# Transposing an fp32 state in one pass and splitting it out of PSUM, in place of transposing its two fp16 halves

## The reference

```python
state = x
for _ in range(5):
    s_in = state @ in_W.T + in_b
    s_out = state @ out_W.T + out_b
    a = concatenate([adj @ s_in, adj.T @ s_out, state])
    r = sigmoid(a @ r_W.T + r_b)
    z = sigmoid(a @ z_W.T + z_b)
    joined = concatenate([adj @ s_in, adj.T @ s_out, r * state])
    h_hat = tanh(joined @ h_W.T + h_b)
    state = (1 - z) * state + z * h_hat
out = tanh(state @ o1_W.T + o1_b) @ o2_W.T + o2_b
return layernorm(x + out)
```

## Time and profile before

| | us |
|---|---|
| median of 3 runs | 1097.2 (1095.56 to 1097.23) |
| profiled execution, first to last instruction (its span) | 1094.1 |
| median less span | 3.1 |
| TensorE busy | 1070.0 |
| VectorE busy | 582.4 |
| ScalarE busy | 249.8 |
| GpSimd busy | 22.4 |

### The profile page before, as it was taken

One profiled execution on the slowest core, in us unless ns is written; L12 is line 12 of the kernel. 1 busy time (PEld: TensorE's weight loads), 2 busy tenths in 40 slices (PEclk: granted clock), 3 DMA queues, 4 the chain that ended last, 5 costly groups with the idle time before them and its releaser, 6 DMA issues.

```text
span 1094.1 us, 12578 instructions
## 1 busy us (share of the span) xinstructions
PE 1070.0 (98%) x5160; PEld 497.1 (45%) x5160; DVE 582.4 (53%) x1024; ACT 249.8 (23%) x314; POOL 22.4 (2%) x27
## 2 busy tenths in 40 slices
PE   6999999999999999999999999999999999999994
PEld 3444444444444444444444444444444444444442
DVE  5944478854443536271726262635445363747466
ACT  3666322221211111121112112112121121111111
POOL 0300000020000000000000000000000000101000
PEclk9999999999999999999999999999999999999998
DMA  9989100010000000000000000000000000101000
GB/s 339 398 309 398 67 1 1 1 39 1 1 1 1 1 1 1 2 1 1 1 1 1 1 1 2 1 1 1 1 1 1 1 1 1 39 1 39 1 20 19
DMA packets 13638, 46.30 MB, mean 42 GB/s; under 512 B 1168, under 2 KB 7952, under 8 KB 9488
## 3 DMA queue, kind: packets, MB, share of 16 engines
q1 hardware_dynamic: 13584, 45.49, 10.9%
HBM read 43.39 MB, written 2.10 MB: 42 GB/s over the span
## 4 chain that ended last, share of the span: by engine, by line
PE 95%; DVE 2%; DMA 1%; SPq 1%; ACT 1%; issue 0%; DVEq 0%
PE bank L646 50%; PE bank L724 42%; PE bank L737 1%; DMA tmp<-in_adj 1%; PE bank L766 1%; PE bank L748 1%; SPq L196 0%; DVE deg_words L477 0%; ACT tmp L307 0%; DVE tmp L502 0%; ACT a L270 0%; DVE pq_words L418 0%; SPq L193 0%; SPq L192 0%; DVE pq_words L574 0%
## 5 line engine op out<-in xcount | busy, mean ns | idle before, releaser
L724 PE MATMUL bank<-pq_words,w 128*128 128x512 f16 x1440 | 327.6, 379 | 0.0
L646 PE MATMUL bank<-a,state_n 128*128 128x512 fp8e4 x1280 | 280.8, 379 | 3.3 <-ACT a L270 3.3
L646 PE MATMUL bank<-at_words,state_n 128*128 128x512 fp8e4 x1280 | 282.0, 379 | 0.2
L418 DVE SCALAR_TENSOR_TENSOR pq_words<-bank,pq_words 128x512 f16<-128x512 f32 x80 | 55.2, 691 | 350.2 <-ACT pq_words L297 328.1
L724 PEld LDWEIGHTS bank<-pq_words,w 128*128 128x128 f16 x1440 | 140.8, 98 | 168.3
L646 PEld LDWEIGHTS bank<-at_words,state_n 128*128 128x128 f16 x1280 | 124.6, 98 | 149.4 <-issue 1.1
L646 PEld LDWEIGHTS bank<-a,state_n 128*128 128x128 f16 x1280 | 124.3, 98 | 150.0 <-issue 3.9
L307 ACT ACTIVATE tmp<-tmp,bias_sb,scal 128x512 f32<-128x512 f32 x120 | 97.3, 813 | 394.4 <-DVE tmp L502 394.4
L724 PE MATMUL bank<-split_t,w 128*128 128x512 f16 x480 | 116.7, 379 | 0.6 <-DVE deg_words L477 0.6
L502 DVE TENSOR_TENSOR tmp<-bank,tmp 128x512 f32<-128x512 f32 x120 | 82.5, 689 | 57.4 <-PE bank L724 56.6
L297 ACT ACTIVATE pq_words<-bank 128x512 f16<-128x512 f32 x64 | 38.2, 597 | 315.0 <-PE bank L646 315.0
(11 more groups left out here) (90 smaller groups left out, 383.2 us busy)
## 6 DMA issues: line engine op xcount, KB each, us to landing
tmp<-in_adj SPq DMA_DIRECT2D x16, 1024.0 KB, 6.8
tmp<-in_adj_t SPq DMA_DIRECT2D x16, 1024.0 KB, 6.9
pq_words<-in_gate_w SPq DMA_DIRECT2D x6, 384.0 KB, 6.1
at_words<-in_x SPq DMA_DIRECT2D x4, 512.0 KB, 8.4
state_t<-in_x_t SPq DMA_DIRECT2D x4, 512.0 KB, 7.7
pq_words<-in_x SPq DMA_DIRECT2D x4, 512.0 KB, 4.2
out<-pq_words SPq DMA_DIRECT2D x8, 256.0 KB, 2.3
deg_words<-in_io_w SPq DMA_DIRECT2D x4, 128.0 KB, 4.0
```

The costliest lines, as they stand in the source:

```text
L418: return nc.vector.scalar_tensor_tensor(pq[:, c, q, 1, :], src[:, :], PSC, pq[:, c, q, 0, :], ALU.mult, ALU.subtract).then_inc(done, 1)
L646: return nc.tensor.matmul(dst[:, :], state_n[:, j, part, feat(f)], adj8[:, j, cols(c)], start=j == 0 and part == 0, stop=j == JT - 1 and p ...
L724: last = nc.tensor.matmul(dst[:, :], w16[:, k, wp, feat(gi)], rhs, start=i == 0 and (wp, xp) == PASSES[0], stop=i == KT - 1 and (wp, xp) = ...
```

## The change

Each group of 8 fp16 transposes becomes 4 fp32 transposes of `state_t` itself, with a new fp32 identity `ident32`, into the same bank, read as 128x512 in fp32 (`tr32`). ScalarE makes the hi half out of the bank, with the scale. A new VectorE instruction, `nat_lo`, makes the lo half out of the bank and the hi half, and counts the new semaphore `s_natl`. TensorE's waits move from `s_sl` to `s_new` and from `s_nat` to `s_natl`. On VectorE `nat_lo` stands: at the start of steps 1 to 4 (both feature tiles of chunk 3), behind `pq_lo` 0 and 1 of chunks 1 to 3 in steps 1 to 3, and in the first step's chunks 1 to 3 between `gate_pre` and `update` of gate tiles 4 and 5. GpSimd makes `ident32` with one copy.

```diff
+        ident32 = sb("ident32", [P, P], F32)
...
-        tr16 = tr_bank[:, :].bitcast(F16).rearrange("p (j s f) -> p j s f", j=JC, s=2)
+        tr32 = tr_bank[:, :].rearrange("p (j f) -> p j f", j=JC)
...
+            pool.wait_ge(s_const, 2)
+            nc.gpsimd.tensor_copy(ident32[:, :], ident[:, :]).then_inc(s_id32, 1)
...
             def nat_out(n, c, f, direct):
                 dst = state_n if direct or c == CH - 1 else next_n
                 act.wait_ge(s_tr, 2 * n + f + 1)
-                nc.scalar.copy(dst[:, c * JC:(c + 1) * JC, :, feat(f)], tr16).then_inc(s_nat, 1)
+                nc.scalar.activation(dst[:, c * JC:(c + 1) * JC, 0, feat(f)], tr32, ACT.Identity, scale=SIG) \
+                    .then_inc(s_nat, 1)
...
-            def gates(n, c):
+            def nat_lo(n, c, f, direct):
+                dst = state_n if direct or c == CH - 1 else next_n
+                rows = dst[:, c * JC:(c + 1) * JC, :, feat(f)]
+                dve.wait_ge(s_nat, 2 * n + f + 1)
+                nc.vector.scalar_tensor_tensor(rows[:, :, 1, :], tr32, SIG, rows[:, :, 0, :],
+                                               ALU.mult, ALU.subtract).then_inc(s_natl, 1)
+
+            def gates(n, c, between=False):
...
                 for f in range(FT):
                     gate_pre(n, 2 * FT + f)
+                    if between:
+                        nat_lo(n - 1, c - 1, f, True)
                     update(n, c, f)
...
-            def step(t, last):
+            def step(t, last, first_direct):
                 for c in range(CH):
                     n = CH * t + c
+                    if c == 0:
+                        nat_lo(n - 1, CH - 1, 0, first_direct)
+                        nat_lo(n - 1, CH - 1, 1, first_direct)
                     pq_lo(n, 0)
+                    if c > 0 and not last:
+                        nat_lo(n - 1, c - 1, 0, False)
...
                     pq_lo(n, 1)
+                    if c > 0 and not last:
+                        nat_lo(n - 1, c - 1, 1, False)
...
-                        dve.wait_ge(s_nat, 2 * n)
+                        dve.wait_ge(s_natl, 2 * n)
...
             for c in range(CH):
-                gates(c, c)
+                gates(c, c, between=c > 0)
...
             def transposes(n, c, f):
-                pe.wait_ge(s_sl, FT * n + f + 1)
+                pe.wait_ge(s_new, FT * n + f + 1)
                 if isinstance(n, int) and n == 0 and f == 0:
                     pe.wait_ge(s_deg, 2 * CH)
+                    pe.wait_ge(s_id32, 1)
                 else:
-                    pe.wait_ge(s_nat, 2 * n + f)
+                    pe.wait_ge(s_natl, 2 * n + f)
                 for j in range(JC):
-                    for part in range(2):
-                        last = nc.tensor.transpose(tr16[:, j, part, :],
-                                                   split_t[:, part, f, c * CW + j * P:c * CW + (j + 1) * P],
-                                                   ident[:, :])
+                    last = nc.tensor.transpose(tr32[:, j, :],
+                                               state_t[:, f, c * CW + j * P:c * CW + (j + 1) * P],
+                                               ident32[:, :])
                 last.then_inc(s_tr, 1)
...
                     if c == 0:
-                        pe.wait_ge(s_nat, 2 * n)
+                        pe.wait_ge(s_natl, 2 * n)
...
-            pe.wait_ge(s_nat, 2 * (CH - 1))
+            pe.wait_ge(s_natl, 2 * (CH - 1))
             start_step(CH - 1)
```

More of the change, by code:

```diff
@@ L137, in gnn_program @@
         s_cast = sem("s_cast")
-        s_const0, s_const = sem("s_const0"), sem("s_const")
+        s_const0, s_const, s_id32 = sem("s_const0"), sem("s_const"), sem("s_id32")
         s_mx, s_mall = sem("s_mx"), sem("s_mall")
@@ L155, in gnn_program @@
         s_sh, s_sl = sem("s_sh"), sem("s_sl")
-        s_tr, s_nat = sem("s_tr"), sem("s_nat")
+        s_tr, s_nat, s_natl = sem("s_tr"), sem("s_nat"), sem("s_natl")
         s_cur = sem("s_cur")
@@ L624, in _ @@
             for c in range(CH):
-                gates(c, c)
+                gates(c, c, between=c > 0)
             with dve.Fori(1, STEPS - 1) as t:
-                step(t, False)
-            step(STEPS - 1, True)
+                step(t, False, True)
+            step(STEPS - 1, True, True)
         @block.tensor
```

## The result

The changed kernel takes 1109.12 us (median of 4 runs, 1106.82 to 1110.06) against 1097.12 us: 1.011 times the kernel before, 95% interval 1.0095 to 1.0124. It is slower by 12.0 us. The forecast was 1104.5 us, 7.4 us slower: the direction and the range held, the size was 4.6 us short. The profiled execution has a span of 1106.7 us and took 1108.51, so 1.8 us lie around a span. The 3.1 us that the forecast put there for the kernel before also held 1.3 us by which its profiled execution was shorter than the median.

The account below looks back on a forecast made before the run. The prediction took TensorE to bound the kernel: 7.9 us of first-step waits plus 29 x (0.43 - 0.45) gave +7.3 us on a 1094.1 us span, 1101.4, and with 3.1 around it 1104.5 us; range 1097.5 to 1117.5.

Parts of the forecast that it names:

- The 3.1 us: Time around the profiled span: the median of the runs was put 3.1 us above the 1094.1 us span.
- TensorE as the bound: TensorE holds 95% of the chain; each nanosecond its transposes take or it waits there is a nanosecond of the kernel.
- Part 1: Transposes on TensorE: a group of 4 fp32 ones takes 0.43 us against 0.45 for 8 fp16; 29 groups count.
- transpose mode four times faster for fp32: Cited for the cheap-transpose rival: 54 ns per fp32 transpose, no more than an fp16 one; 1098.4 us, chance 0.18.
- Part 2: ScalarE and VectorE in steps 1 to 4: VectorE gets 22 us more work, none of it on the path.
- Part 3: First step's gates: TensorE waits for `nat_lo` four times, 2.56, 1.87, 1.87 and 1.64 us, 7.9 us in sum.
- Nor should the granted clock fall in a wait of 2.5 us: First step's waits: TensorE keeps the full 2.4 GHz clock, as 19 matmuls did after 3.30 us of idling.
- The forecast's own range of 1103 to 1106 us: Range around the main case of 1104.5 us, which was given chance 0.56.
- the stated range: 1097.5 to 1117.5 us, from just under the cheap-transpose case to the upper end of the dear-transpose case.

Follow-up runs that it names:

- e2_double: e1_early with each group of four fp32 transposes issued twice; 1110.31 us, 1.0117 times the kernel before.
- e3_fp16_wait: Kernel before, keeping fp16 transposes, with a VectorE copy of the lo half at each place of `nat_lo`, TensorE waiting for it; 1103.43 us, 1.0063 times the kernel before.
- e0_again: The changed kernel run again, unchanged, on a second chip; 1106.69 us, 1.0098 times the kernel before.
- e4_first_only: Changed kernel with only the first lo half of each of the first step's chunks made earlier; 1103.51 us, 1.0060 times the kernel before.
- e6_copy_only: Kernel before with only GpSimd's copy of the identity to fp32 added, which nothing reads; 1097.11 us, 1.0004 times the kernel before.
- e1_early: Changed kernel with the first step's lo halves made earlier on VectorE, second hi half earlier on ScalarE; 1099.72 us, 1.0035 times the kernel before.
- e8_early_again: e1_early run again, for a second profile and more timed runs; 1100.21 us, 1.0025 times the kernel before.

## Why the prediction was right in direction and short in size

- TensorE as the bound: right. From `start_step` to the last gate tile the time follows the transposes' price alone, -0.42 us measured, 26 x (0.435 - 0.45) = -0.39. One reading was loose: the last transposes of the earlier trace rows start at 869.5, 0.5 us behind the stretch of the earlier trace rows; nothing hangs on it.
- Part 1, the price of an fp32 group: right, 0.44 us for 0.43. Four transposes of a row take 0.60 us with a tail of 0.27, so one comes each 0.11 us, twice an fp16 one. The loads last 140 ns and don't set the pace: in e2_double 8 of them take 1.01 us, 0.12 from start to start, so that they overlap. By the Trainium skill, page "TensorE: Matmul & The Clock Gate", section "Weight-path perf modes — Fast Weight Load (FWL) and DoubleRow", fp32 gets no fast load. The 140 against 98 ns fit that, but the group was not bound by it. The Trainium skill, page "TensorE: Matmul & The Clock Gate", section "Terms", has transpose mode four times faster for fp32. Taken against two passes as L641's products are made in, the rows show half: 0.11 us, where two passes of 128 columns are 0.217 us, an estimate from L641's 256 columns.
- Part 2, no cost from the second step on: right. 270 to 881 us has 0.14 us of idle time.
- Part 3, the four waits: right in place, releaser and size, 2.60, 1.98, 1.99 and 1.67 us for 2.56, 1.87, 1.87 and 1.64. `nat_lo` took 0.75, not 0.69 us; `nat_out` took 0.68, within the 0.60 to 0.81.
- The step that failed: "Nor should the granted clock fall in a wait of 2.5 us". It was read from a single row in which the clock had held behind 3.30 us of idling. In the profile after it fell behind 2.45 us in the first step (1.7 us lost), behind 3.75 at the start (1.7 us) and behind 2.74 at the end, in e3_fp16_wait behind 2.11; in e0_again it held behind 2.46. The length of the idle time doesn't decide it: at the start it fell behind 2.08 us (e4_first_only) and held behind 3.49 (e6_copy_only). Whether it falls differs from run to run, and I had left the term out instead of bounding it. The forecast's own range of 1103 to 1106 us failed by it; the stated range held because it was made wide for the price of the transposes, which wasn't what was off.
- That term is also where the 12 us differ from 7.4: of the 5.3 us by which the span was over its forecast, 0.3 us are the waits' size, 0.2 the smaller saving on the groups, and 4.8 the three stretches at the lower clock, less the small shifts of start and end beside them. The runs bear out that it is a matter of what follows idle times, since holding TensorE busy at the ends took 2.5 to 3.6 us off e1_early. Why the changed kernel falls more often at the ends than the kernel before, with TensorE's order there the same, stays open. If the mean clocks of the timed runs mean what those of the profiles do, it is the end above all: all 7 runs of e8_early_again are at 0.993, but 50 of 70 of the kernel before at 0.996 or more. It is not the identity's copy (e6_copy_only). It doesn't need fp32 transposes: e3_fp16_wait's profile has none and its last 24 head products take 5.17 us. Nor does it grow with their number, as far as four runs of e2_double tell (0.994 to 0.998).
- Not foreseen for the experiments: moving `nat_lo` ahead doesn't take its wait away for free. VectorE is busy for 88 of 124 us in the earlier trace rows, but in the gates alone for 26.0 of 30 us (200 to 230 us, the kernel before), and comes late to work put ahead. e1_early and e4_first_only both show it.

## What to carry to other kernels

Look up what stands ahead of the releasing instruction in its own engine's order: here `nat_lo` stood behind an instruction that waits for TensorE's newest work, and so TensorE had to wait for its own. A form that is covered in the long steps can be exposed in the short one; use it where it is covered. TensorE's idle times of 2.1 to 4.3 us cost themselves and, in some runs, about 1.7 us more in the matmuls behind; give that its own term, with 0 and 1.7 us as its bounds for each.

## What the runs showed of the hardware

- An fp32 transpose of 128x128 takes 0.11 us on TensorE in a row, an fp16 one 0.056: one fp32 pass is worth two fp16 transposes, to 3%. Its weight loads last 140 ns each and overlap when 8 follow each other (1.01 us, e2_double).
- Behind idle times of 2.1 to 4.3 us TensorE worked at half rate for some us in some executions and not in others of the same kernel (2.46 held in e0_again, 2.45 fell in the changed kernel's profile), at about 1.7 us lost for each. The granted clock reads 0.50 within such a stretch (1090 to 1093 us) and 1.00 from 245 to 1083 us. With a few matmuls of no use in the idle times of the ends, all but one of 32 runs had a mean clock of 0.997 or 0.998.
- VectorE copies 128x512 in fp16 out of PSUM in 0.42 us; with an fp32 bank, a scalar out of SBUF and a second operand it takes 0.75 us, and 0.69 with a constant scalar.
